# Rows for the batch attention normed and transposed inside the linear attention

## The reference

```python
def _layernorm(x, axis=-1, eps=1e-05):
    m = jnp.mean(x, axis=axis, keepdims=True)
    v = jnp.var(x, axis=axis, keepdims=True)
    return (x - m) / jnp.sqrt(v + eps)

x = x + _L0_attn_ref(_layernorm(x, axis=-1), L0_attn_w_qkv, L0_attn_w_out, L0_attn_b_out)   # linear attention
x = x + _L0_ffn_ref(_layernorm(x, axis=-1), L0_ffn_ln1_weight, L0_ffn_ln1_bias, ...)        # "batch attention" + experts

# _L0_attn_ref: 16 heads of 64
q = jax.nn.softmax(q, axis=-2) * SCALE        # over the 64 features of a head
k = jax.nn.softmax(k, axis=-1)                # over the 32 positions
context = jnp.einsum('bhdn,bhen->bhde', k, v)
out = jnp.einsum('bhde,bhdn->bhen', context, q)

# _L0_ffn_ref begins with a second layer norm of the rows it is given, with weight and bias,
# then attention in which the 128 batches are the sequence
ln1 = _layer_norm(hidden_states, ln1_weight, ln1_bias)
```

## Time and profile before

| | us |
|---|---|
| median of 3 runs | 2163.9 (2162.57 to 2165.39) |
| the profiled execution | 2159.83 |
| its span, first to last instruction | 2157.6 |
| PE busy | 1989.1 (92%) |
| DVE, ACT, POOL busy | 1567.2, 1263.4, 1178.0 |
| linear attention | from 107.6 to 495.4 |
| deviations, norm and transpose | from 495.7 to 512.0 |
| batch attention begins | 512.3 |

### The profile page before, as it was taken

One profiled execution on the slowest core, in us unless ns is written; L12 is line 12 of the kernel. 1 busy time (PEld: TensorE's weight loads), 2 busy tenths in 40 slices (PEclk: granted clock), 3 DMA queues, 4 the chain that ended last, 5 costly groups with the idle time before them and its releaser, 6 DMA issues. The chain is left out here.

```text
span 2157.6 us, 79866 instructions
## 1 busy us (share of the span) xinstructions
PE 1989.1 (92%) x26981; PEld 1475.4 (68%) x26982; DVE 1567.2 (73%) x5614; ACT 1263.4 (59%) x3636; POOL 1178.0 (55%) x1218
## 2 busy tenths in 40 slices
PE   8899999997999888869999999999789999989998
PEld 5577777774677667747777777777456666665897
DVE  7888888883777773558989898989667667654444
ACT  5555555554888523527777777777545555542332
POOL 3234344442888636637777777777266666634231
PEclk9999999997999979979999999999899999979999
DMA  7630000000000002311111111111220000000113
GB/s 229 205 126 0 0 0 0 0 1 1 1 0 0 1 19 63 91 72 39 38 37 37 37 37 37 37 37 59 102 83 0 0 0 0 0 2 31 39 48 99
DMA packets 48112, 86.63 MB, mean 40 GB/s; under 512 B 8608, under 2 KB 34208, under 8 KB 47392
## 3 DMA queue, kind: packets, MB, share of 16 engines
q1 hardware_dynamic: 42896, 74.84, 10.8%
q0 software_dynamic: 5120, 10.55, 1.5%
HBM read 72.73 MB, written 18.48 MB: 42 GB/s over the span
## 5 line engine op out<-in xcount | busy, mean ns | idle before, releaser
L2575 ACT ACTIVATE xat_scores<-xat_scores,xat_least 128x257 f32<-128x257 f32 x512 | 258.5, 505 | 84.3 <-DVE xat_least L2716 84.0
L2716 DVE CUSTOM_DVE_ANT_0 xat_scores<-bank,xat_mask_b 128x257 f32<-128x257 f32 x512 | 202.7, 419 | 51.4 <-PE bank L2421 45.3
L1109 POOL TENSOR_TENSOR gqa_rnorm<-gqa_norm_min,gqa_minus_half 128x12 f32<-128x12 f32 x64 | 145.8, 2278 | 104.7 <-DVE gqa_norm_min L1186 104.7
L2477 PE MATMUL bank<-ident,xat_scores 128*128 128x128 f32 x1024 | 189.7, 288 | 0.2 <-DVE xat_p_T L2723 0.2
L753 POOL TENSOR_TENSOR lin_q_softmax<-lin_q_exp,lin_q_rsum 128x512 f32<-128x512 f32 x64 | 66.7, 1042 | 223.4 <-DVE lin_q_rsum L814 223.4
L2477 PEld LDWEIGHTS bank<-ident,xat_scores 128*128 128x128 f32 x1024 | 116.2, 142 | 81.9 <-issue 43.8
L1427 POOL TENSOR_TENSOR bat_scores<-bat_scores,bat_max 128x512 f32<-128x512 f32 x128 | 130.4, 1040 | 32.6 <-DVE bat_max L1459 32.6
L1459 DVE CUSTOM_DVE_ANT_0 bat_scores<-bank,bat_causal_add 128x128 f32<-128x128 f32 x512 | 110.7, 286 | 47.2 <-PE bank L1315 47.2
L631 PEld LDWEIGHTS bank<-lin_w_v_out,lin_z_T 128*128 128x128 f32 x1024 | 119.1, 191 | 22.0 <-issue 20.2
L631 PE MATMUL bank<-lin_w_v_out,lin_z_T 128*128 128x128 f32 x1024 | 131.2, 281 | 1.3 <-ACT lin_z_T L683 1.3
L2621 POOL TENSOR_TENSOR xat_p_rsum_wide<-xat_p_rsum,xat_head_of_row 128x128 f32<-128x128 f32 x128 | 51.1, 400 | 146.2 <-DVE xat_p_rsum L2729 146.2
(11 more groups left out here) (361 smaller groups left out, 6019.9 us busy)
## 6 DMA issues: line engine op xcount, KB each, us to landing
glu_ctx_N<-in_ctxN SPq DMA_DIRECT2D x32, 576.0 KB, 3.7
xat_ctx_T<-in_ctxT SPq DMA_DIRECT2D x32, 516.0 KB, 3.5
xat_pad<-in_xat_pad SPq DMA_DIRECT2D x32, 128.5 KB, 3.3
expert_w<-in_glx_w SPq DMA_DIRECT2D x1, 4096.0 KB, 15.8
moe_rows<-in_moe_empty SPq DMA_DIRECT2D x1, 3120.0 KB, 15.4
moe_slot_row<-moe_rows SPq DMA_DIRECT2D x48, 65.0 KB, 1.9
slot_rows<-in_empty_rows SPq DMA_DIRECT2D x1, 2580.0 KB, 11.1
slt_rows<-slot_rows SPq DMA_DIRECT2D x40, 64.5 KB, 1.8
```

The lines of the kernel that those rows point to most:

```text
L1109: pool.tensor_tensor(rn[h][:, :], sm[h][:, :], half_neg[:, :], ALU.pow).then_inc(rnorm, 1)
L2477: m = pe.transpose(dst[:, c * P:(c + 1) * P], sx[j % 2][:, g, c * P:(c + 1) * P], k.ident[:, :])
L2575: act.activation(sx[j % 2][:, g, :], sx[j % 2][:, g, :], ACT.Exp, bias=mn[j % 2][g][:, 0:1], scale=-1.0, accum_out=sm[j % 2][:, g:g + 1]). ...
L2716: dve.tensor_tensor_reduce(sx[j % 2][:, g, :], pS[g][:, 0:J], mb[slot][:, j, :], 1.0, BIG, ALU.add, ALU.min, mn[j % 2][g][:, 0:1]).then_in ...
```

## The change

The norms, transposes and copies for the batch attention are made inside the linear attention, for tile t - 3 in the body of tile t; the stages ln3 and ln3b go. `residual_tile` is taken apart so that DVE aggregates each tile's statistics at once; POOL makes the two factors of a tile with a power of -0.5 (`deviations`), DVE norms the rows (`rows_norm`, after the subtraction of q's maximum in h = 0), PE transposes them (`n_transpose`, next to the transpose of x) and ACT copies them (`n_copy`). The last four tiles follow after the last product y, with four warming products ahead of the last transpose. In the batch attention the four warming products before the first `front` are gone, and of the six after the scores three are left and stand behind the second `front`. The factor for the rows that are kept (`k.SHIFT`) is made by DVE at the start of the batch attention. The load of the weight and bias of the norm moves one stage up.

```diff
@@ stage_linear_attention, PE
+            def n_transpose(t, at):
+                pe.wait_ge(normed_twice, t + 1)
+                pe.transpose(pN[:, MC], nr[at][:, :], k.ident[:, :]).then_inc(n_turned, 1)
...
                     if h == 0 and not last:
                         x_transpose(t + 1, 1 - slot)
+                    if h == 0 and not last and since(t, 3):
+                        n_transpose(t - 3, 1 - slot)
...
                     y(t, slot, 1)
+                    pe.wait_ge(z_copied, 2 * BT * NT)
+                    for i in range(4):
+                        wait(pe, n_copied, t - 3 + i)
+                        n_transpose(t - 3 + i, (1 - slot, slot, 2, 3)[i])
+                        if i == 2:
+                            for c in range(4):
+                                pe.matmul(pQ[:, :], k.ident[:, :], w[:, 0, 0, :], start=True, stop=True)
@@ ACT
+            def n_copy(t):
+                act.wait_ge(n_turned, t + 1)
+                act.activation(k.LT[:, t, :], pN[:, MC], ACT.Identity, bias=wb[:, 1:2], scale=wb[:, 0:1]).then_inc(n_copied, 1)
...
                     if h == 0 and not last:
                         x_copy(t + 1, 1 - slot)
+                    if h == 0 and not last and since(t, 3):
+                        n_copy(t - 3)
@@ POOL
+            def deviations(t, slot):
+                pool.wait_ge(moments, t + 1)
+                pool.sem_inc(pool_waited, 1)
+                pool.tensor_scalar(var1[slot][:, :], mv[slot][:, 1:2], 1.0, EPS, ALU.mult, ALU.add).then_inc(vars_made, 1)
+                pool.tensor_scalar(var2[slot][:, :], mv[slot][:, 1:2], 1.0 + EPS, EPS * EPS, ALU.mult, ALU.add).then_inc(vars_made, 1)
+                pool.tensor_copy(k.MV[:, t, :], mv[slot][:, :]).then_inc(kept, 1)
+                pool.wait_ge(vars_made, 2 * t + 1)
+                pool.tensor_tensor(k.RSTD[:, ts(t, 1)], var1[slot][:, :], half_neg[:, :], ALU.pow).then_inc(rstds_made, 1)
+                pool.wait_ge(vars_made, 2 * t + 2)
+                pool.wait_ge(kept, t + 1)
+                pool.tensor_tensor(r2[slot][:, :], var2[slot][:, :], half_neg[:, :], ALU.pow).then_inc(rstds_made, 1)
...
+                if since(t, 3):
+                    deviations(t - 3, 1 - slot)
                 pool.wait_ge(normed, t + 1)
                 pool.tensor_tensor(k.X[:, t, :], k.X[:, t, :], bo[:, :], ALU.add).then_inc(biased, 1)
@@ DVE
+            def rows_norm(t, slot, at):
+                dve.wait_ge(rstds_made, 2 * t + 2)
+                dve.sem_inc(dve_waited, 1)
+                dve.tensor_scalar(nr[at][:, :], k.X[:, t, :], mv[slot][:, 0:1], r2[slot][:, 0:1],
+                                  ALU.subtract, ALU.mult).then_inc(normed_twice, 1)
...
                     dve.tensor_tensor(qs[h][:, :, :], q3, spread(qm[h][:, :], DH), ALU.subtract).then_inc(qshift, 1)
+                    if h == 0 and since(t, 3):
+                        rows_norm(t - 3, 1 - slot, 1 - slot)
                     dve.wait_ge(k_made, u + 1)
...
-                    aggregate(dve, k, added, 2 * NT - 4, 0, NT - 2)
-                    add(t - 1)
-                    add(t)
+                    add(t - 1, 1 - slot)
+                    rows_norm(t - 2, slot, slot)
+                    rows_norm(t - 1, 1 - slot, 2)
+                    add(t, slot)
+                    rows_norm(t, slot, 3)
@@ stage_batch_attention, PE
                 if first:
-                    warm_up(pe, k, pO, 4)
                     pe.wait_ge(ones_set, 4)
                     front(s, slot)
                 scores(s, slot)
-                if first:
-                    warm_up(pe, k, pO, 6)
-                else:
+                if not first:
                     p_transpose(s - 1, 2)
                     p_transpose(s - 1, 3)
                 if not last:
                     front(s + 1, 1 - slot)
+                if first:
+                    warm_up(pe, k, pO, 3)
@@ build
-                deviation_phase(nc, k, "ln3", twice=True)
-                stage_norm_transpose(nc, k, "ln3b", k.X, k.AT, ln_b, hidden=True)
```

More of the change, by code:

```diff
@@ L478, in spread, with stage_linear_attention @@
     return ap.unsqueeze(2).broadcast_to([ap.shape[0], ap.shape[1], n])
-def stage_linear_attention(nc, k, w, wo, bo, ahead):
+def stage_linear_attention(nc, k, w, wo, bo, wb, ahead):
     H, DH = 16, 64
@@ L517, in stage_linear_attention @@
         rk = [sb(f"k_rsum{i}", [P, NC * BT]) for i in range(2)]
+        half_neg = sb("minus_half", [P, 1])
+        bns = [sb(f"x_stats{i}", [P, 6]) for i in range(2)]
+        mv = [sb(f"x_moments{i}", [P, 2]) for i in range(2)]
+        var1, var2 = ([sb(f"{n}{i}", [P, 1]) for i in range(2)] for n in ("var_once", "var_twice"))
+        r2 = [sb(f"rstd_twice{i}", [P, 1]) for i in range(2)]
+        nr = [sb(f"rows_normed{i}", [P, D]) for i in range(4)]
         pQ, pK, pY, pQT = k.bank[0:4]
@@ L540, in stage_linear_attention @@
         y_made, pe_waited = sem("y_made"), sem("pe_waited")
+        half_set, moments, vars_made, rstds_made = sem("minus_half_set"), sem("moments"), sem("vars_made"), sem("rstds_made")
+        dve_waited = sem("dve_waited")
+        kept, normed_twice, n_turned, n_copied = (sem(n) for n in (
+            "moments_kept", "rows_normed_twice", "rows_transposed", "rows_copied"))
         added = sem("residual_chain")
@@ L547, in third, with since @@
             return not isinstance(t, int) or t >= 2
+        def since(t, n):
+            return not isinstance(t, int) or t >= n
         @block.sync
@@ L731, in body @@
                     z_copy(t, slot, 1)
+                    for i in range(4):
+                        n_copy(t - 3 + i)
             steps(act, NT, body)
@@ L756, in body @@
                     k_norm(unit(t, 1), 1)
+                    for i in range(3):
+                        deviations(t - 2 + i, (slot + i) % 2)
             steps(pool, NT, body)
@@ L765, in norm, with add @@
                                   ALU.subtract, ALU.mult).then_inc(normed, 1)
[L767 removed]
+            def add(t, slot):
                 dve.wait_ge(y_made, t + 1)
                 dve.wait_ge(biased, t + 1)
[L770 removed]
+                dve.tensor_tensor(k.X[:, t, :], k.X[:, t, :], pY[:, 0:D], ALU.add).then_inc(added, 1)
+                dve.wait_ge(added, 2 * t + 1)
+                dve.sem_inc(dve_waited, 1)
+                dve.bn_stats(bns[slot][:, :], k.X[:, t, :]).then_inc(added, 1)
+                dve.wait_ge(added, 2 * t + 2)
+                dve.sem_inc(dve_waited, 1)
+                dve.bn_aggr(mv[slot][:, :], bns[slot][:, :]).then_inc(moments, 1)
+            def rows_norm(t, slot, at):
+                dve.wait_ge(rstds_made, 2 * t + 2)
+                dve.sem_inc(dve_waited, 1)
+                dve.tensor_scalar(nr[at][:, :], k.X[:, t, :], mv[slot][:, 0:1], r2[slot][:, 0:1],
+                                  ALU.subtract, ALU.mult).then_inc(normed_twice, 1)
             def k_sum(u, h):
@@ L1288, in stage_batch_attention @@
         staged, f_made, kept = sem("ln_staged"), sem("qkv_made"), sem("rows_kept")
+        shifted = sem("shifts_made")
         qk_copied, v_copied, k_spread = sem("qk_copied"), sem("v_copied"), sem("k_spread")
@@ L1384, in keep_row @@
             def keep_row(t):
+                if isinstance(t, int) and t == 0:
+                    act.wait_ge(shifted, 1)
                 act.activation(k.HID[:, t, :], k.X[:, t, :], ACT.Identity, bias=k.SHIFT[:, ts(t, 1)],
@@ L1468, in body @@
             def body(s, slot, first, last):
+                if first:
+                    dve.scalar_tensor_tensor(out=k.SHIFT[:, :], in0=k.MV[:, :, 0], scalar=-1.0, in1=k.RSTD[:, :],
+                                             op0=ALU.mult, op1=ALU.mult).then_inc(shifted, 1)
                 for g in range(G):
```

17 lines of the change are left out of this document (9 added, 8 removed).

## The result

The changed kernel took 2145.72 us (median of 4 runs, 2144.32 to 2149.27), the kernel before 2163.24 on the same chip (4 runs, 2160.33 to 2165.39): 0.9926 of it, 95% interval 0.9912 to 0.9941. It is faster, by 17.5 us where 9.9 were forecast. The time lies outside the 2149 to 2159 that the forecast called its own, 0.7 us inside the lower end of the range of 2145 to 2162, and next to the 2145.6 of rival (a). Run again on another chip beside other kernels it took 2146.39 (6 runs) against 2161.12 (11 runs): 0.9929, 0.9915 to 0.9944.

A forecast was written before the change was run, and what follows sets the result against it. PE was taken as the bound, busy 92%, with savings only where it idles or is slowed. Handover and clock -21.4, transposes +3.1, norm's collision +8.4: -9.9 us, from 2163.9 to 2154.0; own range 2149 to 2159, wider 2145 to 2162.

The forecast's parts named there:

- rival (a): Loop: POOL's five instructions take 1.7 or more, or less than 1.1, so no collision; 2145.6 us; 22%.
- (1): End of linear attention: without ln3 and ln3b, POOL starts the batch attention 6.3 after y, not 17.8; gain 11.5 us.
- (2): Start of batch attention: second scores 9.5 us after its start instead of 19.6; gain 10.1 us.
- the signs: Batch attention: second scores expected 9.5 to 11.3 us after POOL's start, among the marks to check in the changed profile.
- (3): Batch attention's start: second to third scores at full clock, gain 1.1 us; clock falling before first scores costs 1.3.
- (4): Loop, PE: 28 added transposes at 0.11 each cost 3.1 us, all paid.
- (5): Loop, ACT: one added copy per tile, 0.45 us, costs nothing because ACT waits there.
- (7): Loop, DVE: added aggregation and norm of rows; the norm, in a chain with slack 0.24, costs 8.4 us.
- (6): Loop, POOL: two variances, a copy, two powers estimated at 1.45 us, plus copy of rows and k norm; hidden.
- The term of 8.4: Loop, DVE: norm of rows held by POOL's k norm, 0.30 us a tile over 28 tiles, 8.4 us.
- rival (d): Handover gives only about half, as tile 31's chain or DVE's first maxima are late; 2163 us; 6%.

The follow-up runs named there:

- where nothing collides: Changed kernel with POOL's variances and powers made earlier, in h = 1; norm of rows left in place (2142.94 us) or put ahead of q's maximum (2143.61 us).
- the changed kernel with the old warming: Changed kernel with the ten earlier warming products (four, then six) put back in the batch attention: 2151.85 us, 0.9965 of the kernel before.
- idle reductions: Kernel before with one or two unused DVE reductions behind q's subtraction in h = 0: 2161.99 us (1.000) with one, 2181.67 us (1.0092) with two.
- one power: Changed kernel without the first of POOL's two powers in the loop: 2146.00 us, 0.9926 of the kernel before.
- both moved: Changed kernel with POOL's variances and powers made earlier, in h = 1, and the norm of rows ahead of q's maximum: 2143.61 us, 0.9923 of the kernel before.

## Why the prediction was right, and where it was not

**Right: the handover, (1) and (2).** Every step of it can be laid on the rows: rounds of 0.83 and 0.88 for the transposes (0.8), a start at 6.18 (6.3), first scores at 3.71 (3.7), second at 10.58 (9.5 to 11.3). The second profile has 12.20 for the last, outside the signs, with the clock at 0.50 for longer:

```profile
514.00:516.00 2.00, 0.39 (x4) 0.39 (x8) 0.00 (x0) 0.46 (x2) 1.37 (x2) 0.81 0.00 0
516.00:518.00 2.00, 2.00 (x9) 0.50 (x6) 0.12 (x1) 0.00 (x0) 0.00 (x0) 0.50 0.00 0
518.00:520.00 2.00, 2.00 (x8) 1.48 (x8) 2.00 (x21) 0.41 (x2) 1.10 (x2) 0.50 0.00 0
520.00:522.00 2.00, 2.00 (x4) 0.94 (x3) 1.35 (x14) 1.61 (x3) 2.00 (x3) 0.50 0.00 0
```

**Right: the clock, (3).** It fell to 1.2 GHz in both profiles after a stretch in which PE did little (some 0.95 us of work from 510 to 514 in the first). The first scores took 2.09 for 1.14; the front and the head of the warming were slowed too. From y to the third scores the sum had -21.4; the profiles show -21.5 and -20.2.

**Right: the transposes, (4).** 3.1 forecast, 3.35 measured where nothing collides. **Right: ACT, (5),** at nothing: where nothing collides, no growth is left for it.

**Wrong: the slack in (7).** This is the step that failed: "So a softmax may end 0.56 after the next q begins. ... the slack is 0.24 us." It may end 0.90 after it and the slack is 0.58. With PE's own 0.11 it was 0.69 in the changed kernel. The chain was delayed by 0.27 for the norm and 0.49 for the collision, 0.76: 0.07 over, of which the trace shows 0.05 as a later start and 0.06 as a longer transpose, in one tile of two. The term of 8.4 was 1.9 (2.5 with tile 31). The prediction named its own sign for this: its main step is wrong if the loop's growth isn't in PE's wait for the q softmax. Of the 0.17 a tile 0.12 is the transposes, and only 0.05 goes with that wait.

**Wrong in size: POOL's five instructions, (6).** 1.45 was the estimate. From the end of the q softmax (302.02) to the bias (303.80) are 1.78, of which 0.08 lie before the first variance: about 1.7. The k norm stood 1.65 after the start of the q softmax before (343.65 - 342.00) and stands 3.47 after it now (304.45 - 300.98), 1.8 later. So in the tile that doesn't follow the branch it came after the norm of the rows, which is the bound where it costs nothing.

**The collision: size right, tile wrong.** The size of a stall was right: forecast to end 1.13 after POOL's start, found at 1.13. Which tile has it was not: 0.87 was forecast for the tile that doesn't follow the branch and 0.50 for the other, and they were 0.36 and 0.83. With the measured 1.8 both come out: the k norm starts 0.3 before the norm in one kind (315.71, 316.01) and 0.47 after it in the other (304.45, 303.98).

**Luck: the time of rival (a).** Its condition, 1.7 or more for POOL's five, was met, but it asked that the instructions pass each other in every tile, and in half of them they don't. It had 3.1 for the linear attention, which grew by 7.4. The three stretches that the change touches bring 2163.9 to 2149.9 or 2151.1; that the median came out at 2145.7 is owed to the 3.5 us and more that can't be put to a place. It is luck too that the range of 2145 to 2162 still holds it. In rival (d) a sum is off: half of 21.4 kept, with 11.5 in the loop, gives 2164.7 and not 2163.

**Not foreseen.** The linear attention grew by 7.4: 5.3 in the loop, 0.6 in tile 31, as above, and 1.6 by the clock near its end (tile 31 took 25.2 us, and 23.6 in the changed kernel with the old warming, which had full clock there). In the changed kernel the granted clock was 0.50 from 497.28 to 500.69, and a product y took 3.58, where its like before, at 488.45, took 2.05:

```profile
497.02 3.58 PE L649 MATMUL bank<-lin_w_v_out,lin_z_T 128*128 128x128 f32 x16
```

This dip stands in both profiles of the changed kernel and in both with idle reductions, and in none of the other ten. What decides it is not shown.

The Trainium skill says in "SBUF — State Buffer", section "Who interferes with whom", that the loser blocks until the winner's whole instruction is over. Here the norm, which takes 0.35 alone, ended 1.13 after POOL's start in each collision of the changed kernel. If it needs its 0.35 once it is let go, it began 0.78 after that start, 0.27 before the end of POOL's record of 1.05. So the rows agree that one waits for the other, and not that it waits to the end of the record, as the earlier trace rows had it.

## What to carry to other kernels

To learn how late an operand may come, don't read it off the wait that stands before its reader: look for the same gap where the operand was early, and if the gap is still there it is the reader's own. Then put one and two dummy instructions of known length into the chain of the old kernel; two runs gave the slack to 0.05 us here. And a delay on a chain with slack is worth what is over the slack, so two instructions that exclude each other can cost less than the stall they show. The stall also shifts what follows, so the next tile may be spared, as with one power here.

## What the hardware showed that was not expected

- The first scores of the batch attention ran at 1.2 GHz in each profile with the new warming products, with four, two or none of them ahead of the last transpose (2.09 us; in one profile, of the kernel with both moved, half of them, 1.36); with the old four ahead of `front` they ran at 2.4 (1.14 us). Between the old four and the first scores PE had `front` and one wait of 1.73; between the new four and the first scores it had two waits, 1.91 and 1.73.
- When the clock came back varied by 3.3 us between two executions of the same program (13.1 us after the last product y in one, 16.3 in the other), and with it the third scores by 1.3 us.
- Making POOL's work 0.5 us shorter made more tiles collide (three of four for one of two), and two tiles 0.14 us longer (23.90 for 23.76).
